# The projection's bias joins the residual's x on POOL instead of the middle rows on VectorE: a cross-attention and expert block on one core

## The reference

```
a   = layernorm(x)                                 # LN 1
o   = (softmax(q1 k1) - lambda * softmax(q2 k2)) v  # 16 heads, 77 context rows a batch
x   = x + rms_norm(o) * norm_w @ proj_w.T + proj_b  # the "middle rows"
h   = layernorm(x)                                  # LN 2
x   = x + sum over the 2 chosen of 8 experts of weight * (silu(g) * u) @ down.T
```

## Time and profile before

| what | value |
|---|---|
| time of three runs | 552.91, 556.72, 558.14 us (median 556.72) |
| span of the profiled execution, first to last instruction | 555.4 us |
| mean granted TensorE clock | 0.963 |
| busy: PE, DVE, ACT, POOL | 89%, 70%, 61%, 49% |
| chain that ended last, by engine | PE 67%, DVE 10%, ACT 7%, DMA 5% |

### The profile page before, as it was taken

One profiled execution on the slowest core, in us unless ns is written; L12 is line 12 of the kernel. 1 busy time (PEld: TensorE's weight loads), 2 busy tenths in 40 slices (PEclk: granted clock), 3 DMA queues, 4 the chain that ended last, 5 costly groups with the idle time before them and its releaser, 6 DMA issues.

```text
span 555.4 us, 12114 instructions
## 1 busy us (share of the span) xinstructions
PE 495.3 (89%) x3741; PEld 363.6 (65%) x3756; DVE 386.1 (70%) x805; ACT 340.2 (61%) x642; POOL 273.4 (49%) x347
## 2 busy tenths in 40 slices
PE   4695889998999888799798999999999999999990
PEld 3463546775666555526566888878888888777750
DVE  5437458888888765788577997887667677666551
ACT  1220588888788888374675777766656566645530
POOL 5006464574564564203227566656567555644244
PEclk9986799999999989899999999999999999999996
DMA  7567757768658632563666777967555465554224
GB/s 215 191 171 174 239 147 231 203 171 264 192 170 253 200 118 76 179 204 112 152 137 111 158 129 195 180 120 157 94 104 86 85 84 101 96 68 77 30 30 47
DMA packets 88090, 79.89 MB, mean 144 GB/s; under 512 B 49176, under 2 KB 73368, under 8 KB 87896
## 3 DMA queue, kind: packets, MB, share of 16 engines
q1 hardware_dynamic: 76512, 63.38, 41.8%
q0 software_dynamic: 11520, 15.74, 17.6%
HBM read 49.08 MB, written 22.41 MB: 129 GB/s over the span
## 4 chain that ended last, share of the span: by engine, by line
PE 67%; DVE 10%; ACT 7%; DMA 5%; issue 5%; SPq 3%; POOL 2%; another core or an unknown queue 0%; ACTq 0%; POOLq 0%
PE bank L1459 27%; PE bank L1476 13%; PE bank L1242 5%; PE bank L1288 4%; DMA x_parts<-WE 3%; PE bank L1274 3%; PE bank L1488 2%; PE bank L1256 2%; PE bank L1311 2%; PE bank L1324 2%; DVE FB L1165 2%; PE bank L1297 2%; DVE FB L1169 2%; ACT FB L876 2%; PE bank L1336 2%
## 5 line engine op out<-in xcount | busy, mean ns | idle before, releaser
L1459 PE MATMUL bank<-FB,WE 128*128 128x0 bf16 x1440 | 187.6, 280 | 2.6 <-issue 1.0
L1459 PEld LDWEIGHTS bank<-FB,WE 128*128 x1440 | 136.1, 98 | 34.9 <-issue 4.3
L709 POOL DMA_INDIRECT out<-FB,slot_tok x60 | 99.9, 1665 | 91.2 <-DVE FB L1186 85.4
L876 ACT ACTIVATE FB<-FB 128x512 bf16<-128x512 f32 x120 | 75.6, 630 | 69.9 <-DVE FB L1165 63.8
L1169 DVE TENSOR_TENSOR FB<-FB 128x512 bf16<-128x512 f32 x120 | 83.3, 694 | 46.9 <-ACT FB L876 43.0
L1476 PE MATMUL bank<-FB,WE 128*128 128x0 bf16 x720 | 103.7, 280 | 4.3 <-DVE FB L1169 2.2
L1165 DVE TENSOR_TENSOR FB<-FB,bank 128x512 f32<-128x512 f32 x120 | 81.9, 683 | 27.8 <-ACT FB L870 21.5
L700 POOL DMA_INDIRECT FB<-x_parts,slot_tok x60 | 61.7, 1028 | 68.0 <-DMA FB<-FB 26.7
L870 ACT ACTIVATE FB<-bank 128x512 f32<-128x512 f32 x120 | 70.7, 589 | 33.9 <-PE bank L1459 29.3
L1476 PEld LDWEIGHTS bank<-FB,WE 128*128 x720 | 67.6, 98 | 23.5 <-issue 7.8
L633 POOL TENSOR_TENSOR WE<-FB,WE 128x256 bf16<-128x256 f32 x104 | 67.8, 678 | 22.1 <-ACT WE L740 22.0
(11 more groups left out here) (180 smaller groups left out, 616.4 us busy)
## 6 DMA issues: line engine op xcount, KB each, us to landing
FB<-w SPq DMA_DIRECT2D x26, 512.0 KB, 5.5
WE<-w SPq DMA_DIRECT2D x44, 256.0 KB
WE<-q_parts SPq DMA_DIRECT2D x32, 200.0 KB
WE<-x SPq DMA_DIRECT2D x16, 256.0 KB, 5.2
q_parts<-FB SPq DMA_DIRECT2D x32, 128.0 KB
x_parts<-WE SPq DMA_DIRECT2D x20, 128.0 KB, 4.0
out<-WE SPq DMA_DIRECT2D x20, 128.0 KB, 5.5
q_parts<-WE SPq DMA_DIRECT2D x16, 128.0 KB
```

The source lines that it names most:

```text
L709: pool.indirect_dma_start(out=out, out_offset=bass.IndirectOffsetOnAxis(ap=slot_tok[:, c:c + 1].bitcast(U32), axis=0), in_=result_tile(c), ...
L876: nc.scalar.activation(hT[k % 3][:, 0, :], hid[k % 2], ACT.Copy).then_inc(hi_ready, 1)
L1459: ins = nc.tensor.matmul(to, wf[:, bass.ds(at + o, P)], xgT[s % 2][:, 2 * part + kc, :].shape_from_register(long[s % 2]), start=(z == 0), ...
```

## The change

The add of the bias leaves the middle rows. A new kind `XB` on POOL adds the broadcast bias to `xd` in place, a tile at a time, once the load of x has landed; `P1` reads that sum and is now the last writer of the middle rows, so its semaphore is `xm_ready`, and `xm1_ready` is gone. `P2` keeps the statistics only. In POOL's table the two entries stand behind `L 3` and ahead of `RS 0`. The next batch's `XD`, and PE's reuse of the projection's bank, now wait for `xm_ready` in the place of `xm1_ready`; both were and are incremented by `P1`.

```diff
         POOL_PLAN = (
...
-            ("L", 3, 0), ("RS", 0, 3), ("L", 4, 0), ("L", 5, 0), ("L", 6, 0), ("L", 7, 0), ("RS", 1, 3), ("RM", 0, -1), ("L", 8, 0))
+            ("L", 3, 0), ("XB", 0, -1), ("XB", 1, -1), ("RS", 0, 3), ("L", 4, 0), ("L", 5, 0), ("L", 6, 0), ("L", 7, 0), ("RS", 1, 3), ("RM", 0, -1), ("L", 8, 0))
...
                 if kind == "XD":
                     if b > 0:
-                        sp.wait_ge(xm1_ready, TPB * b)
+                        sp.wait_ge(xm_ready, TPB * b)
...
+                if kind == "XB":
+                    if b == 0 and i == 0:
+                        pool.wait_ge(smalls_in, 16 * 9)
+                    if i == 0:
+                        pool.wait_ge(xd_in, 16 * (b + 1))
+                    nc.gpsimd.tensor_tensor(xd[:, i, :], xd[:, i, :], bias_bc, ALU.add).then_inc(xb_ready, 1)
...
                 if kind == "P1":
                     dve.wait_ge(pj_mm, n + 1)
                     dve.wait_ge(rms_ready, n + 1)
-                    dve.wait_ge(xd_in, 16 * (b + 1))
+                    dve.wait_ge(xb_ready, n + 1)
...
-                                                   op0=ALU.mult, op1=ALU.add).then_inc(xm1_ready, 1)
+                                                   op0=ALU.mult, op1=ALU.add).then_inc(xm_ready, 1)
                 if kind == "P2":
-                    dve.wait_ge(xm1_ready, n + 1)
-                    nc.vector.tensor_tensor(xmid[:, i, :], xmid[:, i, :], bias_bc, ALU.add).then_inc(xm_ready, 1)
                     dve.wait_ge(xm_ready, n + 1)
...
-                    product(oT, oT_ready, n, pj_sb, D, pj_mm, bank_no(kind, n), xm1_ready)
+                    product(oT, oT_ready, n, pj_sb, D, pj_mm, bank_no(kind, n), xm_ready)
```

More of the change, by code:

```diff
@@ L272, in moe_attention_kernel @@
         xd_in = sem("xd_in")
-        xm1_ready = sem("xm1_ready")
+        xb_ready = sem("xb_ready")
         xm_ready = sem("xm_ready")
```

## The result

The changed kernel takes **621.31 us** (median; 616.07 to 622.17) where the kernel before, run beside it, takes 557.03 us (552.91 to 561.86): a ratio of 1.112, 95% interval 1.1084 to 1.1155. It is 64 us slower. The profiled execution has a span of 619.3 us (before 555.4) and a mean granted clock of 0.912 (before 0.963). Two executions, 604.76 us among the twelve of experiment 11 and 563.91 us among those of the kernel before, ran at a lower granted clock than the others (0.829 and 0.946) and are left out of the ratios.

A forecast was written before the change was run, and what follows sets the result against it. The prediction took PE as the full engine in attention, with waits between queues deciding. It summed 26.8 + 14.8 + 8.4 - 0.4 = 49.6 us over the 555.4 us span, giving 606 us on the median, range 581 to 620.

The forecast's parts named there:

- What is removed: Sixteen DVE bias adds, 7.8 us, mostly becoming DVE idle time; only the last add comes off the end, -0.4 us.
- The adds on POOL: Sixteen adds put on POOL at 0.67 us each, 1.34 a pair; their work as such hidden in POOL's idle time.
- The wait and its place: POOL behind L 3 waits for x to land, 9.8 us of standstill in step 4, holding the work queued behind.
- (1) The LayerNorm chain: RS 0 and RS 1 behind the wait delay LN, MX 4 and PE's SC 6 in steps 1 to 4: 26.8 us.
- (2) The weight chain: L 4 to 7 behind the wait delay W 0, H 0, E 10 and S 12; steps 5 and 6 cost 14.8 us.
- Steps 7 and 8: The attention part's last two steps, with neither LN nor W 0 behind the wait: counted as nothing.
- The clock: Half clock on PE after each of six new pauses of 6 to 7 us, 1.4 us each: 8.4 us.
- the first pair of the earlier trace: PE idle 24.3 to 28.6, then 2.6 us half clock; the second: idle 227.9 to 230.2, then 6.5 us.
- Only the LayerNorm queue: Rival: only LN's delay counts, later weight loads are absorbed and PE's clock stays 1.0; 583 us, chance 0.17.
- The clock stays low for long: Rival: half clock after PE's pauses costs 19.5 us in place of 8.4; 617 us, chance 0.13.
- Faster: Rival: x lands before POOL reaches XB, so at most 7.8 us of DVE adds come off; 549 us, chance 0.03.
- Hidden: Rival: the wait slides into POOL's 4.09 us pause before RM 0, nothing measurable; about 557 us, chance 0.05.

The follow-up runs named there:

- experiment 11: Changed kernel with two tiles for x, its load issued one step earlier, adds still behind L 3: 558.09 us, ratio 0.9992 to the kernel before.
- experiment 4: Kernel before without the 16 bias adds on either engine, so the output lacks the projection's bias: 555.79 us, ratio 0.9962.
- experiment 12: Changed kernel with two tiles for x, loaded one step earlier, and the adds behind RS 1: 557.13 us, ratio 0.9970 to the kernel before.
- experiment 1: Changed kernel with the two POOL adds and their wait moved behind RM 0, ahead of L 8: 558.36 us, ratio 0.9992 to the kernel before.
- experiment 2: Kernel before plus a POOL wait for x and a one-column write behind L 3, bias add left on VectorE: 606.62 us, ratio 1.0871.
- experiment 3: Kernel before plus 16 unused POOL adds, two a step behind L 3, waiting for no load: 559.10 us, ratio 1.0012.
- experiment 5: Changed kernel with RS 0 and RS 1 moved ahead of the wait for x: 596.22 us, ratio 1.0681 to the kernel before.
- experiment 9: Changed kernel with RS 0, RS 1 and RM 0 moved ahead of the wait for x: 602.62 us, ratio 1.0796 to the kernel before.
- experiment 6: Changed kernel with L 4 to 7 moved ahead of the wait for x: 593.79 us, ratio 1.0637 to the kernel before.
- experiment 7: Changed kernel with 12 unread matmuls ahead of SC 6 in each of steps 1 to 4: 614.16 us, ratio 1.1002 to the kernel before.
- experiment 8: Changed kernel with 14, 15, 20 and 16 unread matmuls ahead of SC 6 in steps 1 to 4: 610.21 us, ratio 1.0932 to the kernel before.
- experiment 10: Changed kernel with the load of x issued first behind the shift transfers in SP's queue: 576.01 us, ratio 1.0319 to the kernel before.

## Why the prediction was right, and where its sizes were off

The forecast was 606 us and slower; it came out slower, at 621.3, 1.3 us above the range of 581 to 620. The mechanism held; two terms of the sum did not: the clock behind a pause was priced too low, and steps 7 and 8 were put at nothing. By its own steps:

- **What is removed** was put at -0.4 us. Experiments 4 and 12 give 0.7 to 3.5 and 0.1 to 3.2 us. A little more of VectorE's time shows than the last add; where, no run here separates.
- **The adds on POOL** were put at 1.34 us a pair; they take 1.40 to 1.60, 749 ns each (page, L689). The estimate from the Trainium skill, GPSIMD Engine Reference, section 3.1, was 562 ns; the measurement decides, and no run here shows so small a figure. Its section 4.1 (VectorE first for two-input work, GpSimd about two times slower) fits: VectorE takes 0.42 us for the same add at its shortest.
- **The wait and its place.** Forecast 9.8 us of standstill in step 4, measured 9.95; over steps 1 to 6 it is 8.3 to 12.9. Right, and experiments 1, 2, 3 and 11 show that the wait at this place is the cause: alone it costs 48 us of the 64, and without it the adds at the same place cost at most 1.7.
- **(1) The LayerNorm chain.** Landing to SC 6 forecast 6.73 us, measured 6.9. SC 6 starts 12.95, 11.87, 12.39 and 12.58 us after the issue of x in steps 1 to 4, before 6.45, 4.84, 4.92 and 5.29: late by 6.5, 7.0, 7.5 and 7.3, together 28.3 us against 26.8. Right.
- **(2) The weight chain.** Steps 5 and 6 were to be 14.8 us longer and 2.8 for the clock; they are 15.7 longer: near in sum, but made of other parts, and so in part by luck. In step 5 H 0 waits as forecast, yet PE pauses twice, 3.18 us before OT 1 (RM 0 and P1, the chain that was not followed) and 2.44 before S 12 (H 0):

```profile
223.03 0.41 PE L1308 MATMUL bank<-identf,WE 128*128 128x128 f32 x2 [3.18 <-DVE WE L1026]
...
227.30 0.65 PE L1278 MATMUL bank<-WE 128*77 128x256 bf16 x2 [2.44 <-ACT WE L771]
```

  For steps 1 to 4 the prediction says that this chain "gives about as much as (1)". It gives less: without the LayerNorm chain these steps lose 20.8 us in experiment 5 and 27.6 in experiment 9, with the LayerNorm chain, shorter by 2.6 us a step, and not this one 34.0 (experiment 6), of 43.4 in the changed kernel.
- **"Steps 7 and 8 have neither LN nor a W 0 behind the wait. I count nothing for them."** This step failed. Step 7 is 5.5 us longer. RM 0 stands behind XB too, and it is there in every step; in step 7 it holds DVE's P1 and with it PE's OT 1. POOL:

```profile
269.61 1.42 POOL L689 TENSOR_TENSOR WE<-WE 128x256 f32<-128x256 f32 x2 [7.22 <-DMA WE<-x]
...
274.08 0.55 POOL L657 TENSOR_TENSOR WE<-WE 128x1 f32<-128x1 f32 x1
```

DVE:

```profile
274.72 0.48 DVE L1026 SCALAR_TENSOR_TENSOR WE<-bank,WE 128x256 f32<-128x256 f32 x1 [2.77 <-POOL WE L657]
```

PE:

```profile
275.35 0.66 PE L1308 MATMUL bank<-identf,WE 128*128 128x128 f32 x2 [2.67 <-DVE WE L1026]
```

  P1 starts 11.2 us after the issue of x where it took 7.7 (212.60 - 204.93), so 3.6 us late. Behind the pause the clock is slow again, 0.60 on average over 7.7 us (275.3 to 283.0); that the rest of the 5.5 is due to it no run here shows.
- **The clock** was mis-sized, and this is the largest part of the miss. I took 1.4 us a pause, because PE is dense behind the pause as after the first pair of the earlier trace rows and, so I wrote, not after the second. The rows do not say that: PE is busy 2.60 of 2.60 us in the first pair and 6.37 of 6.50 in the second, so I had no ground for the cheaper one. What comes on top of the late SC 6 in steps 1 to 4 is 43.4 - 28.3 = 15.1 us, 3.8 a step, and experiments 7 and 8 put 2.1 to 4.1 of it (3.2 on average) on the clock. That is 4 x (3.2 - 1.4) = 7.2 us more than I took, of the 14.3 between the forecast sum and the measured spans. The rest of the 3.8, about half a microsecond a step, is not separated. That PE has dense work behind a pause did not bring its clock back as soon as after the first pair: it was at 0.50 for 7 to 9 us after PE had started again, where the forecast had 2 to 4. The second pair of the earlier trace rows, 3.25, comes near the 3.2. But the kernel before has a third pause, which I did not read, nearly as long as those of the forecast and with far more half clock behind it:

```profile
41.30:46.70 5.40, 0.01 (x1) 0.00 (x0) 3.67 (x11) 0.60 (x1) 2.20 (x6) 0.99 0.58 165
46.90:63.20 16.30, 13.29 (x52) 8.59 (x53) 8.60 (x19) 3.57 (x5) 10.88 (x31) 0.50 0.73 206
```

  By the working of the prediction this third pair gives up to 8 us a pause, less where PE is not dense (it is busy 13.29 of the 16.30 us). So the rows of before bound the price far less closely than 1.3 to 3.25 us, and that the second pair comes so near is in part luck.

The sum again: 49.6 forecast, + 1.5 (SC 6 later), + 9.5 (behind the pauses of steps 1 to 4), - 1.9 (steps 5, 6), + 5.5 (step 7), - 0.3 (end) = 63.9, the difference of the two spans.

The rivals. *Only the LayerNorm queue* (583) does not hold: experiment 5 leaves it out and still loses 39 us, and what it would be alone, experiment 6, is 594. *The clock stays low for long* (617) was right on its point. *Faster* (549) had the right condition, x there in time, and the wrong price: with that condition met (experiments 11 and 12) the time is 0.997 to 0.999 of before. *Hidden* falls; it needs the adds later in the queue, which is experiment 1.

## What to carry to other kernels

In this kernel an instruction on an engine with idle time cost next to nothing by its length (experiment 3), but its wait was paid by whatever stood behind it in that queue. Before work is moved, look when its input lands, follow every kind of work behind the new place to its consumer (also the small ones), and either put the new work where the input is already there or make the input earlier. Where a new pause falls on TensorE, read what the clock did behind every pause that the trace has, and carry the whole spread into the range instead of the mildest price. Moving a load up in its queue moves others down; look who waits for those.

## What the runs showed of the hardware that was not expected

- *The clock behind a short pause.* With 12 matmuls of filling, PE was idle for 1.45 and 2.13 us in steps 1 and 3 and kept a granted clock of 1.00; after 1.97 and 2.69 us in steps 2 and 4 it fell to 0.50. With the longer fill, it fell after 1.66 us in step 4. The length of a single pause did not decide it in these runs.
- *VectorE and POOL at the same time.* The same DVE add (L1019, both inputs in SBUF) takes 0.42 us alone and 0.74 to 0.97 where POOL's adds or its L run at the same time, and POOL's pair takes 1.60 instead of 1.40. In step 5 of the changed kernel:

```profile
211.51 0.42 DVE L1019 TENSOR_TENSOR WE<-WE 128x256 f32<-128x256 f32 x1
...
217.35 0.97 DVE L1019 TENSOR_TENSOR WE<-WE 128x256 f32<-128x256 f32 x1
```

and POOL beside it:

```profile
217.30 1.60 POOL L689 TENSOR_TENSOR WE<-WE 128x256 f32<-128x256 f32 x2 [10.07 <-DMA WE<-x]
```

  The Trainium skill, GPSIMD Engine Reference, section 1 (Specifications), says that GpSimd shares its SBUF interfaces with VectorE and contends with VectorE instructions that have two SBUF inputs; these rows agree. Here it costs the kernel next to nothing: in experiment 1 six of the eight pairs took 1.60 or 1.61 us, and its time is level with the kernel before.
- *The same load, 3.1 or 5.7 us.* In step 4 the 256 KB of x landed 3.1 us after their issue where they were the first transfer behind the shifts (experiment 10), and 5.7 us in the changed kernel, where loads and stores of five kinds had been issued right before.
